# Preparing the relation layers of a graph network: which source tiles go first, and in which of the four edge passes

## What is computed

```python
h = relu(layernorm(x)); x = x + sage(h, src, dst, edge_weight, ...)     # weighted neighbour sum, two products, row norm
h = relu(layernorm(x)); x = x + gcn(h, W1, b1, W2, b2, edges)           # two normalised neighbour sums
h = relu(layernorm(x)); x = x + hops(h, edges, edge_weight, W, b)       # h = 0.5*A@h + 0.5*h0, twice; then relu, one product
h = relu(layernorm(x)); x = x + rgcn(h, W0, b0, W1, b1, edges, type)    # two relation layers
# one relation layer, for each of 8 relations r:
xt  = einsum('ni,rio->rno', h, W)              # 8 products of the whole node table
msg = relu(xt[edge_type, src] + b)             # one row of 256 per edge
out = segment_sum(msg, dst)
```

## Time and profile before

| | us |
|---|---|
| median of 3 runs | 2688.56 (2685.17 to 2694.28) |
| the profiled execution, its own time | 2689.72 |
| span of the profiled execution, first to last instruction | 2687.9 |
| TensorE busy | 2387.7 (89%) |
| VectorE busy | 1336.4 (50%) |
| GpSimd busy | 1620.1 (60%) |
| ScalarE busy | 572.3 (21%) |

### The profile page before, as it was taken

One profiled execution on the slowest core, in us unless ns is written; L12 is line 12 of the kernel. 1 busy time (PEld: TensorE's weight loads), 2 busy tenths in 40 slices (PEclk: granted clock), 3 DMA queues, 4 the chain that ended last, 5 costly groups with the idle time before them and its releaser, 6 DMA issues.

```text
span 2687.9 us, 41486 instructions
## 1 busy us (share of the span) xinstructions
PE 2387.7 (89%) x11183; PEld 1798.7 (67%) x11184; DVE 1336.4 (50%) x2819; ACT 572.3 (21%) x1718; POOL 1620.1 (60%) x1701
## 2 busy tenths in 40 slices
PE   7799999999699999999999799998799798766666
PEld 4589999999456588888777477775455555544444
DVE  6788888888676721112373334443344334322232
ACT  1366666666000000000111101111122022000000
POOL 5777777720057777777100377664675757777776
PEclk9899999999799999999999999999899899887887
DMA  3033333322366688553443456653565455333443
GB/s 111 22 118 112 115 115 115 115 114 113 117 191 188 185 315 277 159 180 110 165 148 115 159 161 193 183 159 95 166 184 159 128 154 179 109 103 104 121 120 102
DMA packets 203201, 388.37 MB, mean 144 GB/s; under 512 B 52864, under 2 KB 136942, under 8 KB 202890
## 3 DMA queue, kind: packets, MB, share of 16 engines
q1 hardware_dynamic: 52356, 180.31, 20.0%
q0 software_dynamic: 66944, 111.48, 15.7%
q10 hardware_dynamic: 83718, 94.32, 10.3%
HBM read 244.89 MB, written 141.08 MB: 144 GB/s over the span
## 4 chain that ended last, share of the span: by engine, by line
PE 71%; DVE 10%; issue 8%; POOL 5%; DVEq 2%; ACT 2%; DMA 1%; PEldq 0%; SPq 0%; POOLq 0%; PEld 0%; ACTq 0%
PE agg L1045 16%; PE agg L1166 14%; PE y L922 13%; PE agg L986 9%; PE y L963 5%; POOL gathered L819 5%; PE y L1045 4%; PE agg L1041 4%; PE prod L907 2%; PE y L966 1%; DMA gathered<-table_rel,idx_rel 1%; ACT gathered L1295 1%; DVE onehot L1983 1%; PE y L865 1%; PE turn_ps L892 1%
## 5 line engine op out<-in xcount | busy, mean ns | idle before, releaser
L819 POOL DMA_INDIRECT gathered<-table_rel,idx_rel x840 | 809.4, 964 | 580.4 <-ACTq L1411 258.2
L1166 PE MATMUL agg<-gathered,onehot 128*128 x2072 | 577.3, 435 | 192.4 <-DVE onehot L1983 113.6
L1166 PEld LDWEIGHTS agg<-gathered,onehot 128*128 128x128 f32 x2072 | 434.6, 218 | 328.5 <-issue 262.8
L1983 DVE SCALAR_TENSOR_TENSOR onehot<-iota,keybase,edges 128x256 f32<-128x256 f32 x518 | 240.9, 484 | 642.7 <-PE agg L1166 542.5
L803 POOL DMA_INDIRECT edges_parted<-stream x416 | 402.3, 967 | 179.9 <-issue 126.5
L764 POOL DMA_INDIRECT edges_bucketed<-edges,stream x416 | 401.4, 965 | 148.7 <-issue 122.6
L986 PE MATMUL agg<-h_sb,stream 128*128 128x257 f32 x1250 | 334.9, 392 | 0.0
L1045 PE MATMUL agg<-gathered,stream 128*128 128x256 f32 x1250 | 271.7, 381 | 0.0
L1045 PEld LDWEIGHTS agg<-gathered,stream 128*128 128x128 f32 x1250 | 239.2, 191 | 32.6
L963 PE MATMUL y<-gathered,rel_sb 128*128 128x128 f32 x1300 | 234.8, 290 | 12.6 <-ACT gathered L1295 11.2
L963 PEld LDWEIGHTS y<-gathered,rel_sb 128*128 128x128 f32 x1300 | 218.2, 192 | 36.2 <-ACT gathered L1295 14.4
(11 more groups left out here) (209 smaller groups left out, 2405.3 us busy)
## 6 DMA issues: line engine op xcount, KB each, us to landing
table_rel<-rel_sb ACTq DMA_DIRECT2D x200, 256.0 KB, 3.1
stream<-weights_dense SPq DMA_DIRECT2D x41, 832.0 KB
stream<-weights_dense SPq DMA_DIRECT2D x41, 768.0 KB
weights_dense<-stream SPq DMA_DIRECT2D x25, 832.0 KB, 3.4
stream<-counts_dense SPq DMA_DIRECT2D x50, 416.0 KB
table_rel<-zeros ACTq DMA_DIRECT2D x16, 1280.0 KB
weights_dense<-stream SPq DMA_DIRECT2D x25, 768.0 KB, 3.2
stream<-counts_dense SPq DMA_DIRECT2D x50, 384.0 KB
```

The source lines that it names most:

```text
L819: pool.indirect_dma_start(gathered[:, slot * D:(slot + 1) * D], None, tables[n], bass.IndirectOffsetOnAxis(ap=idx_rel[:, c:c + 1], axis=0) ...
L1166: mm = pe.matmul(agg[b][:, 0:D], onehot[:, place * 2 + k, :], gathered[:, bass.ds(((p + pairs0) & (GP - 1)) * (2 * D) + k * D, D)], start= ...
L1983: nc.vector.scalar_tensor_tensor(onehot[:, place * 2:place * 2 + 2, :], iota[:].unsqueeze(1).broadcast_to([P, 2, P]), keybase[:, bass.ds(t ...
```

## The change

Hop two now takes its tiles in the order 9, 10, ..., 24, 0, ..., 8 (`real_tile`). `EARLY` becomes 16 (tiles 9 to 24) and `LATE = 9` (tiles 0 to 8). In layer one the early edges are those with a source in tiles 9 to 24: 33,589 edges, 66 quads; the late ones 19,536 edges, 39 quads (counted from the inputs). In layer two the nine tiles' edges come first: rel1b makes the products of tiles 0 to 8, rel2a runs over the 39 quads and makes the products of tiles 9 to 24, rel2b runs over the 66 quads. The nine late tiles' half steps run two ahead: three with destination tile 0 of rel1a, then one per tile. The split list is stored a second time, twice in a row, and read back rotated, so that layer two finds the late edges first.

```diff
-    EARLY = 15
+    EARLY = 16
+    LATE = TILES - EARLY
...
-        def step_at(i):
-            return STEPS[(i + 1) // 2], (i + 1) % 2
+        def steps_with(t):
+            halves = range(3) if t == 0 else (t + 2,)
+            return [(EARLY + h // 2, h % 2) for h in halves]
...
-        PRODUCTS = {"hop2": (0, range(TILES)), "rel1b": (1, range(EARLY)), "rel2a": (1, range(EARLY, TILES))}
+        LATE_EDGES = {"rel1a": 0, "rel1b": 1, "rel2a": 1, "rel2b": 0}
+        FIRST_KEY = {"rel1a": 0, "rel1b": TILES, "rel2a": 0, "rel2b": TILES + 1}
+        MADE = {"rel1a": 0, "rel1b": TILES, "rel2a": VISITS, "rel2b": VISITS + TILES - 1}
+        PRODUCTS = {"hop2": (0, range(TILES)), "rel1b": (1, range(LATE)), "rel2a": (1, range(LATE, TILES))}
...
         def real_tile(n, t):
-            return t + EARLY if n == "rel2a" else t
+            if n == "hop2":
+                return (t + LATE) % TILES
+            return t + LATE if n == "rel2a" else t
...
+                    if n == "hop2" and t == 7:
+                        sp.wait_ge(s_kept, 16)
+                        for k in range(2):
+                            sp.dma_start(parted_twice[:, k * RC:(k + 1) * RC, :], kept).then_inc(s_kept, 16)
...
             for pi, n in enumerate(RELS):
+                if pi == 1:
+                    pool.wait_ge(s_keys, 2)
...
-                            bass.IndirectOffsetOnAxis(ap=idx_rel[:, c:c + 1], axis=0)
+                            bass.IndirectOffsetOnAxis(ap=(idx_rel[:], idx_rel2)[pi][:, c:c + 1], axis=0)
...
-                     "rel1a": [(-1, lambda t, b: hop2_step(*step_at(t - 1)), range(TILES))],
+                     "rel1a": [(-1, lambda t, b: hop2_steps(t), range(TILES))],
-                     "rel2a": [(-AHEAD, lambda t, b: relations("rel2a", t, b), range(TILES - EARLY))],
+                     "rel2a": [(-AHEAD, lambda t, b: relations("rel2a", t, b), range(TILES - LATE))],
...
-                          (4, lambda t, b: allow(TILES + EARLY, 0, late), range(EARLY - 1, EARLY))],
+                          (4, lambda t, b: allow(TILES + LATE, late, RQ), range(LATE - 1, LATE))],
...
-            for n in RELS:
+            for n, tiles in zip(RELS, (range(LATE), range(LATE, TILES))):
                 for r in range(REL):
-                    late_rows = tables[n][r * NPAD + EARLY * P:(r + 1) * NPAD].rearrange("(p c) d -> p c d", p=P)
-                    act.dma_start(late_rows, zeros[:].unsqueeze(1).broadcast_to([P, TILES - EARLY, D])).then_inc(s_zeroed, 16)
+                    rows = tables[n][r * NPAD + tiles.start * P:r * NPAD + tiles.stop * P].rearrange("(p c) d -> p c d", p=P)
+                    act.dma_start(rows, zeros[:].unsqueeze(1).broadcast_to([P, len(tiles), D])).then_inc(s_zeroed, 16)
...
+            act.wait_ge(sum_ready, TILES * (DENSE.index("hop2") + 2))
+            act.wait_ge(s_kept, 16 * 3)
+            act.dma_start(kept2, parted_twice[:, bass.ds(late * QUAD, RC), :]).then_inc(s_kept, 16)
             allow(TILES, late, RQ)
...
-            allow(2 * TILES, late, RQ)
+            allow(2 * TILES, 0, late)
...
+                step(nc.vector.tensor_scalar(turned_by[near, 0:1], late_at[near, 1:2], -2.0, None, ALU.mult))
...
+                step(nc.vector.tensor_copy(key_bounds2[near, :], key_groups2[near, :]))
...
+                if n == "rel1b":
+                    dve.wait_ge(s_kept, 16 * 4)
+                    nc.vector.tensor_copy(idx_rel2, kept2[:, :, 1]).then_inc(s_keys, 1)
```

More of the change, by code:

```diff
@@ L471, in static_tiles, with over_tiles @@
                 behind(i)
-        def step_at(i):
-            return STEPS[(i + 1) // 2], (i + 1) % 2
+        def steps_with(t):
+            halves = range(3) if t == 0 else (t + 2,)
+            return [(EARLY + h // 2, h % 2) for h in halves]
         def late_tile(t):
             return EARLY <= t < TILES
-        def over_tiles(eng, visits, parts, first_key, after=(), unrolled=False):
+        def over_tiles(eng, visits, parts, n=None, after=(), unrolled=False):
             all_parts = (*parts, *after)
@@ L499, in turn @@
                     t = tile(-1)
-                    visits(t, (i + 1) % 2, bounds_of(eng, t + first_key, key_bounds))
+                    visits(t, (i + 1) % 2, bounds_of(eng, t + FIRST_KEY[n], key_bounds if n in PASSES[:2] else key_bounds2))
                 for (lag, part, _), now in zip(after, mine[1 + len(parts):]):
@@ L568, in staged_rows @@
         def staged_rows(n, bank):
-            at = (bank + (EARLY if n == "rel2a" else 0)) % 2 * KB
+            at = (bank + (LATE if n == "rel2a" else 0)) % 2 * KB
             return turned[:, at:at + KB, :]
@@ L610, in load_late_blocks @@
                 eng.wait_ge((half_free, sum_ready)[part], TILES * (DENSE.index("hop2") + 1) + t)
-                eng.dma_start(half(0, part), dense(w_dram, t, part)).then_inc(s_stream[0][part], 16)
+                eng.dma_start(half(0, part), dense(w_dram, real_tile("hop2", t), part)).then_inc(s_stream[0][part], 16)
         @block.sync
@@ L679, in stream_blocks @@
                         sp.wait_ge((half_free, sum_ready)[part], at - 1)
-                        sp.dma_start(to(at, part), dense(of, t, part)).then_inc(s_stream[at % 2][part], 16)
+                        sp.dma_start(to(at, part), dense(of, real_tile(n, t), part)).then_inc(s_stream[at % 2][part], 16)
                     if n == "hop2" and t == EARLY - 1:
@@ L911, in relations @@
                 if n == "hop2":
-                    rows = kept_rows(t)
+                    rows = kept_rows(real_tile(n, t))
                 else:
@@ L1139, in hop2_step, with hop2_steps @@
                     rows_product("hop2", s - 1, columns(hopw_t))
+            def hop2_steps(t):
+                for s, half_ in steps_with(t):
+                    hop2_step(s, half_)
             parts = {"hop1": [],
@@ L1157, in visits_of @@
             def visits_of(n):
-                layer, late, tiles0 = PASSES.index(n) // 2, PASSES.index(n) % 2, PASSES.index(n) * TILES
-                pairs0, made0 = layer * RP, layer * VISITS + late * TILES
+                tiles0 = PASSES.index(n) * TILES
+                pairs0, made0 = PASSES.index(n) // 2 * RP, MADE[n]
                 def visit(p, t, b, place, first=False):
@@ L1190, in _ @@
                     pe.sem_inc(S[n, "turned_copied"], 1)
-                if n == "rel2a":
+                if n in ("rel2a", "rel2b"):
                     pe.drain().then_inc(ring_free, 1)
-                over_tiles(pe, visits_of(n), parts[n], TILES * (PASSES.index(n) % 2), unrolled=n == "rel1a")
+                over_tiles(pe, visits_of(n), parts[n], n, unrolled=n == "rel1a")
         @block.scalar
@@ L1864, in hop @@
                     rows_free(n, t)
-                step(nc.vector.tensor_tensor(post[:, 0:D], sums(n, t)[:, 0:D], table(n, t), ALU.add))
+                r = real_tile(n, t)
+                step(nc.vector.tensor_tensor(post[:, 0:D], sums(n, t)[:, 0:D], table(n, r), ALU.add))
                 dve.sem_inc(freed, 1)
@@ L1974, in visits_of @@
             def visits_of(n):
-                layer, late = PASSES.index(n) // 2, PASSES.index(n) % 2
-                free0 = layer * VISITS + late * TILES
+                pairs = kept_pairs if n in PASSES[:2] else kept2_pairs
+                free0 = MADE[n]
                 def visit(p, t, place):
@@ L1993, in visits @@
                                lambda p, place, first=False: visit(p, t, place),
-                               (lambda: hop2_step(*step_at(t - 1))) if n == "rel1a" else None)
+                               (lambda: hop2_steps(t)) if n == "rel1a" else None)
                 return visits
```

68 lines of the change are left out of this document (44 added, 24 removed).

## The result

The changed kernel takes 2692.32 us (median of 20 runs, 2688.53 to 2697.98), the kernel before 2686.72 beside it (20 runs, 2680.72 to 2694.54): ratio 1.0023, 95% interval 1.0015 to 1.0031. The span of its profiled execution is 2693.1 us against 2687.9.

The account below looks back on a forecast made before the run. TensorE (PE) was taken as the bound up to 2275, GpSimd's (POOL) gathers behind it. PE's terms summed to POOL free at 2301.4; 385.5 of gathers, 1 and an 11.9 tail gave span 2699.8, median 2700, range 2693 to 2720.

Parts of the forecast that it names:

- Tiles 16 to 20: In rel1a, the last products without a dense half: 77 us for five tiles, to 1858; POOL's 32.96 us wait goes.
- Bare tiles of rel1a: Tiles 21 to 24, at rel1a's end, now with visits alone: 3 x 11.3 + 5.5 = 39.4 us, to 1897.7.
- 13 bare tiles of rel1b: Tiles with visits alone, 13 instead of seven: 7.9 us each, the short last one 5.5, together 100.3 us.
- The last product tile's visits: In rel2a, after three products ahead and 13 product tiles at 11.45 us; POOL comes free 2 us into them, at 2301.4.
- rel2a's bare tiles behind it: Tiles with visits alone after rel2a's products: 7.7 us each against POOL's 7.5, costing 1 us.
- the price of a bare tile: Tiles with visits alone: some 4 us extra each waiting for VectorE's one-hots, 1.2 us per further visit; 7.9 us in rel1b.
- Rival A: Bare tiles of rel1a and rel1b: VectorE runs ahead, saving 41 us at most, 2659, or half, 2680; 0.20 with Rival B.
- Rival B: Bare tiles on PE's path: the clock stays up, 1.5 us saved per tile over 20 tiles, 2671; 0.20 with Rival A.
- D: Half steps two ahead wait for weights, 1 us in each of 18: 2718; 0.50 together with the forecast and E.
- E: Last product stored over 20 us later than thought, POOL's wait partly returns: below 2705; 0.50 with the forecast and D.
- C: No change, 2690: the first 20 tiles of rel1a priced 5 to 10 us too dear, or bare tiles cost 3 us; 0.30.
- What was costed at nothing: Zero rows (uncovered, 14 us), list's second store and reload (5 each), `key_limits` instructions and a copy (2), moved `allow` in rel1b.

Follow-up runs that it names:

- r3: The changed kernel with ten places for one-hots in place of six, so VectorE can work a bare tile ahead; ratio 1.0003 to the kernel before.
- d1: The changed kernel with TensorE alone loading the two bounds of every destination tile of the relation layers twice; ratio 1.0304 to the kernel before.
- k3: The changed kernel with both bounds of a tile packed in one number, one register load instead of two on every engine; 2677.95 us, 0.9965 of the kernel before.
- p3: The changed kernel with only the first matmul of each relation product in rel2a, the rest left out; ratio 0.9881 to the kernel before.
- e1: The changed kernel with half steps no longer two ahead, one per destination tile of rel1a; ratio 1.0033 to the kernel before.
- d2: The kernel before with TensorE alone loading the two bounds of every destination tile of the relation layers twice; ratio 1.0261 to the kernel before.

## Why the prediction was wrong, point by point

The forecast was 2700 us, +0.43% on its median, with 2693 to 2720 as the likeliest range; measured were 2692.32, +0.23%, which by the bound set there is no change, the side that had 0.33. The structure held: PE is the bound up to the switch, the holes close, bare tiles pay for it. Several terms of the sum were off, and partly cancel.

- *POOL's start*: 1530.3 said, 1532.85 came. Right.
- *rel1a*: tile 3's visits end at 1593.5 (1591 said), twelve tiles to 1783.1 (1781): 15.8 each, right to 0.1. The 33 us wait went. Tiles 16 to 20 took 71.8 us, not 77. The prediction names 27.3 us per two and 0.6 visits more each, which comes to some 72; its 77 holds something more that it doesn't name. In the trace tile 20, the last with products, took 14.6 us, tiles 16 and 18 took 19.4 and 21.2: the hole behind its first visit is 0.58 us, theirs 4.25 and 4.47.
- *Bare tiles of rel1a*: 35.4 us, not 39.4. Around the drain ahead of rel1b and in its first three tiles 2.7 us more went than said. *Nine product tiles*: 102.7, 103.2 said. *13 bare tiles of rel1b*: 95.5, not 100.3. rel1b ends at 2113.7, 10 us before the 2123.7 said.
- *The last product tile's visits* start at 2285.9, where 2299.4 was said: 10 us from rel1b, 3.5 more in rel2a (11.36 a tile where 11.45 was said, the rest at its start).
- *rel2a's bare tiles behind it*: 1 us said, "a shade slower than POOL". They take 7.96 us, and the 64 gathers behind 2289.0 cost 87.4 us where 81.2 is POOL's own pace: 6.2. POOL reached that point at 2289.0, not 2301.4 (-12.4); with 5.2 more for the bare tiles and 0.5 for the rest the net is -6.7: 2693.1, not 2699.8. **The step that failed is the price of a bare tile**, taken as (8.56, less 1.2 a visit), 7.9, from seven tiles with more visits at clock 0.83. The change's own in rel1b, in a longer row, ran at 0.91 for 7.4, and in rel2a, where "a shade slower than POOL" was said, the gap is 2.3 to 2.8 us at 0.84. That made the forecast 8.8 us too dear in rel1a and rel1b and 5.2 too cheap in rel2a. The net of it, 3.6 us, is less than the 5.2 of tiles 16 to 20 and about the 3.5 of rel2a's product stretch. The total came within 7 us in part by luck, since the two errors in this price have opposite signs.
- *Its reason failed outright.* "PE waits at the start of each tile for VectorE's one-hots": r3 had them ready, the gap stayed at 1.76 us, and 0.2% was gained, in rel1a. d1 and k3 show PE's own register loads in its place: 1.3 us of the gap by doubling them, 0.55 to 0.7 us back by halving them. The low clock behind the gap is tied to them in d1 (0.91 to 0.69) but not in k3 (0.91 to 0.92), so how much of it the loads cause is not shown. That other work hides it was right, and d1 shows it: zero in product tiles.
- *Rival A* (the 4 us are not on the path) falls by p3 and d1. *Rival B* (the clock stays up) was right by a little: 0.91 instead of 0.83 in rel1b. *D* (weights late) falls: PE stood still for 2.0 us in all ahead of rel1a's 450 dense matmul records, and the lead alone gained 0.82%. *E*: no wait on L1445 near 1875; 2.13 us even in e1. *C* had the nearest time, 2690, and half of a reason: rel1a up to tile 20 was 3.1 us too dear (C had 5 to 10), but a bare tile's extra in rel1b is 7.39 - 4.0 x 0.9 = 3.8 us, not 3, the visit at full clock as in the row at 2285.93. Of the 3.8, 2.3 are standing still.
- What was costed at nothing stayed at nothing: no row of PE waits for the list's reload or the zero rows.

Not settled: how the 1.3 us divide between the loads and what follows them, and why the clock was 0.91 in one row of bare tiles and 0.83 in the other. What stands in the gap beside the loads (1.7 - 1.3 = 0.4 us in rel1b) was not taken apart.

## What to carry to other kernels

A tile that has only short dependent matmuls behind a register load and a branch pays the load in full, and may pay again in clock: d1 lost 2.65 us a tile for 1.3 us of loads, d2 1.6, and k3 got 0.72 back for half of them. The same instructions are free behind 7 us of queued matmuls. So count such tiles when work is moved between passes; that it is better to spread the long work over all of them than to stack it in a few follows from this, but no run here tests it alone. And where a wait names a releaser, make that releaser early once before believing it: here the gap stayed with the name gone. Look first whether what it names was ready: here the first one-hot was, 2.4 us early.

## What the runs showed of the hardware

- Two register loads from on-chip memory, with what the program puts around them, cost TensorE 1.3 us with an empty queue (d1: gap 1.63 to 2.96 us), nothing with 7 us of matmuls queued (product tile 11.49 us in both).
- The granted clock is lower where there are gaps: 1.00 in product tiles, 0.91 in the changed kernel's bare tiles of rel1b and 0.69 in d1's, which is 62% of the time at 1.2 GHz instead of 2.4. In the window of rel1b's bare tiles, PE stood still for 42.4 of 126 us (3.4 per tile) in d1 and for 28.8 of 91 (2.3) in the changed kernel; the other 1.6 of the 2.65 us that a tile lost are slower matmuls. More gap is not always less clock: d2's row with gaps of 3 us is at 0.81, the kernel before's with 1.7 at 0.83, and k3's with 1.1 at 0.92, no higher than the changed kernel's.
